# The first experts' results scattered to rows by choice and token, and read back by plain loads

## The reference

```python
x = x + L0_gnn(layernorm(x), edges)
xn = layernorm(x)
logits = xn @ gate_w + gate_b
# top 2 of 16 experts per row, weights from the two logits
y[q] = relu(xn @ w1[e_q] + b1[e_q]) @ w2[e_q] + b2[e_q]      # q = 0, 1
x = x + layernorm(xn + weight[0] * y[0] + weight[1] * y[1]) * gamma + beta
x = x + L1_gnn(layernorm(x), edges)
x = x + L1_ffn(layernorm(x))
```

## Time and profile before

| What | us |
|---|---|
| median of three runs | 3184.31 |
| span of the profiled execution (its own time; nothing around it is shown apart) | 3191.6 |
| first expert stage: its block's first work to the next block's | 1068 to 1427 |
| combining stage | 1427 to 1531 |
| second graph layer's aggregation begins | 1531 |
| second expert stage | 2703 to the end |

### The profile page before, as it was taken

The page is one execution under the profiler, slowest core; times in us unless marked ns, Lnnn a source line. Parts: engine busy times, 40 slices in busy tenths (PEclk is TensorE's granted clock), DMA queues, the critical chain, the costliest instruction groups (busy, mean ns, idle before and its releaser), DMA issues. The chain is left out here.

```text
span 3191.6 us, 47669 instructions
## 1 busy us (share of the span) xinstructions
PE 2342.0 (73%) x11533; PEld 1761.9 (55%) x11533; DVE 1710.0 (54%) x4544; ACT 1455.8 (46%) x3766; POOL 1992.3 (62%) x1963
## 2 busy tenths in 40 slices
PE   1549999989998389870366666666676666699997
PEld 1226666667686378660244444444444435599996
DVE  6659898857787500017566565666565655401110
ACT  0247676645564233323544444444444434355553
POOL 1647777667775677755677777777777760133332
PEclk9979999989998599995677776677766767799998
DMA  6657777578886666863777777777777752343223
GB/s 215 230 162 226 229 222 205 173 221 262 252 259 209 219 210 200 250 189 97 209 205 206 205 197 205 205 208 204 203 203 197 203 163 78 103 118 77 61 62 65
DMA packets 361528, 591.11 MB, mean 185 GB/s; under 512 B 81906, under 2 KB 234747, under 8 KB 359136
## 3 DMA queue, kind: packets, MB, share of 16 engines
q0 software_dynamic: 101648, 270.35, 32.0%
q1 hardware_dynamic: 241104, 295.49, 29.0%
q10 hardware_dynamic: 18544, 22.59, 2.2%
HBM read 428.77 MB, written 164.32 MB: 186 GB/s over the span
## 5 line engine op out<-in xcount | busy, mean ns | idle before, releaser
L659 POOL DMA_INDIRECT agg_r_rows<-h_table,parts_and_x x832 | 839.3, 1009 | 290.1 <-issue 217.9
L715 PE MATMUL agg_r_sums<-agg_r_rows,agg_r_onehot 128*128 128x257 f32 x1664 | 674.4, 554 | 382.0 <-DVE agg_r_rows L697 335.3
L715 PEld LDWEIGHTS agg_r_sums<-agg_r_rows,agg_r_onehot 128*128 128x128 f32 x1664 | 414.6, 272 | 624.5 <-issue 542.2
L626 ACT ACTIVATE agg_r_gap<-iota,parts_and_x 128x128 f32<-128x128 f32 x832 | 286.7, 392 | 469.5 <-PE agg_r_sums L715 443.5
L697 DVE TENSOR_TENSOR agg_r_rows<-agg_r_rows,agg_r_rel 128x514 f32<-128x514 f32 x416 | 290.6, 699 | 289.8 <-DMA agg_r_rows<-h_table,parts_and_x 288.4
L688 DVE TENSOR_TENSOR acc<-acc,agg_r_sums 128x257 f32 (+1 forms) x836 | 353.5, 423 | 147.5 <-issue 66.0
L1555 POOL DMA_INDIRECT rl_buf<-r_table,kinds x288 | 320.7, 1114 | 135.3 <-issue 75.4
L1956 PE MATMUL f_pH<-f_xT,f_w 128*128 128x128 f32 x2816 | 352.4, 283 | 36.0 <-DMA f_w<-in_L_ffn_w 24.4
L1956 PEld LDWEIGHTS f_pH<-f_xT,f_w 128*128 128x128 f32 x2816 | 337.3, 197 | 67.8 <-issue 28.3
L2041 ACT ACTIVATE f_hT<-f_pH,f_b 128x128 f32<-128x128 f32 x704 | 198.3, 373 | 298.4 <-PE f_pH L1956 298.0
L1975 PE MATMUL f_pY<-f_w,f_hT 128*128 128x256 f32 x1408 | 326.5, 382 | 8.3 <-DMA f_w<-in_L_ffn_w 8.0
(11 more groups left out here) (406 smaller groups left out, 3404.7 us busy)
## 6 DMA issues: line engine op xcount, KB each, us to landing
agg_r_rel<-relation_rows SPq DMA_DIRECT2D x404, 260.0 KB, 3.3
relation_rows<-rl_buf SPq DMA_DIRECT2D x144, 260.0 KB, 3.1
relation_rows<-rm_buf SPq DMA_DIRECT2D x132, 260.0 KB, 3.4
relation_rows<-f_rr_buf POOLq DMA_DIRECT2D x78, 260.0 KB, 3.2
agg_r_rows<-h_table,parts_and_x POOLq DMA_INDIRECT x832, 3.4
f_w<-in_L_ffn_W SPq DMA_DIRECT2D x18, 512.0 KB, 5.2
f_w<-in_L_ffn_W SPq DMA_DIRECT2D x9, 1024.0 KB, 4.9
f_ys<-f_yb SPq DMA_DIRECT2D x64, 128.0 KB
```

Source lines behind the costliest of these rows:

```text
L626: last = nc.scalar.activation(gap[:, n % HOT, t, :], c.iota[:, 0:P], ACT.Abs, bias=c.tab["b_near"][:, bass.ds(g * 2 + t, 1)])
L659: pool.indirect_dma_start(rows[:, n % SLOTS, t, :], None, table, bass.IndirectOffsetOnAxis(ap=indices[:, t:t + 1], axis=0)).then_inc(s_row ...
L715: last = nc.tensor.matmul(sums[:, (2 * n + t) % BANKS, 0:used], onehot[:, n % HOT, t, :], rows[:, n % SLOTS, t, 0:used], start=True, stop= ...
```

## The change

In the first mixture a slot's result now goes to the row (choice x 3200 + token) of a larger table `ys`, padding slots to rows of their own behind. The row numbers come out of the same matmuls as `token`: the second choice counts tiles from 25 on, and `token` subtracts 3200 again. GpSimd scatters each result with an indirect DMA without addition (`put_rows`), four tiles behind its gather; `yb` has four buffers, and VectorE's loop is written out. SyncE stores nothing any more in that stage. At the end GpSimd waits for its scatters, then does its two last relation stores. `combine_and_norm` reads `got` with twelve plain loads on SyncE ahead of gamma and beta. In both mixtures `home` is made right behind `token`.

```diff
-    ys = c.dram(f"{name}_ys", [NP + P if out is not None else tiles * P, D])
+    ys = c.dram(f"{name}_ys", [NP + P if out is not None else 2 * NP + tiles * P, D])
...
-    FC, Q, Y = nf // P, 4, 4 if out is not None else 2
+    FC, Q, Y = nf // P, 4, 4
...
                 with sp.Fori(1, tiles // 2 - 1) as i:
                     for s in range(2):
                         second(2 * i + s, s)
-                        if out is None:
-                            stored(i, s)
                         first(2 * i + 2 + s, s)
...
-                    hits = [P, NT, tiles]
+                    hits, first = [P, NT, tiles], q * NT if out is None else 0
...
-                v.tensor_scalar(token[:, :], token_f[:, :], 1.0, 0.0, ALU.subtract, ALU.max).then_inc(s_token, 1)
+                if out is None:
+                    v.tensor_scalar(home_f[:, :], token_f[:, :], float(NP), float(-NP), ALU.is_gt, ALU.mult)
+                    st.link(v.tensor_scalar(row_f[:, :], token_f[:, :], 1.0, 0.0, ALU.subtract, ALU.max))
+                    v.tensor_tensor(token[:, :], row_f[:, :], home_f[:, :], ALU.add).then_inc(s_token, 1)
...
+                v.scalar_tensor_tensor(home[:, :], token_f[:, :], -1.0, home_f[:, :], ALU.add, ALU.add).then_inc(s_home, 1)
...
-                    with dve.Fori(0, tiles // 2) as i:
...
+                    for t in range(tiles):
+                        e = dve.value_load(e_tab[0:1, 0, t:t + 1], min_val=0, max_val=ne - 1)
+                        dve.wait_ge(s_y, t + 3)
+                        if t >= Y:
+
+                            dve.wait_ge(s_added[t % Y], 16 * (t // Y))
+                        v.tensor_tensor(yb[:, t % Y, :], pY[t % 2][:, 0:D], b2s[:, bass.ds(e, 1), :].rearrange("p a d -> p (a d)"), ALU.add)\
+                            .then_inc(s_yb, 1)
...
+                def put_rows(t):
+                    pool.wait_ge(s_yb, t + 3)
+                    pool.sem_inc(s_ask, 1)
+                    pool.indirect_dma_start(ys, bass.IndirectOffsetOnAxis(ap=home[:, t:t + 1], axis=0), yb[:, t % Y, :], None).then_inc(s_added[t % Y], 16)
...
+                    if out is None and t >= Q:
+                        if t == Q:
+                            pool.wait_ge(s_home, 1)
+                        put_rows(t - Q)
...
-def gather_results(nc, c, name, k, ys, slot):
...
             @block.gpsimd
             def _(pool):
-                work(pool)
+                pool.memset(k.got[:, :, NT - 1, :], 0.0).then_inc(k.s_rest, 1)
...
             @block.sync
             def _(sp):
+                for i in range(NJ):
+                    full = J if i < NJ - 1 else J - 1
+                    for q in range(2):
+                        at = q * NP + i * J * P
+                        sp.dma_start(k.got[:, q, i * J:i * J + full, :], ys[at:at + full * P, :].rearrange("(t p) d -> p t d", p=P)).then_inc(k.s_got[i], 16)
+                sp.wait_ge(k.s_rest, 1)
+                for q in range(2):
+                    at = q * NP + (NT - 1) * P
+                    sp.dma_start(k.got[0:TAIL, q, NT - 1, :], ys[at:at + TAIL, :]).then_inc(k.s_got[NJ - 1], 16)
                 sp.dma_start(g[:, :], row(I["L0_ffn_gamma"])).then_inc(s_gb, 16)
                 sp.dma_start(b[:, :], row(I["L0_ffn_beta"])).then_inc(s_gb, 16)
...
-                    dve.wait_ge(k.s_got[i], 16 * 2 * J)
+                    dve.wait_ge(k.s_got[i], 32 if i < NJ - 1 else 64)
```

More of the change, by code:

```diff
@@ L1845, in feed_forward @@
             of_slot, two = k.sb(f"{name}_of_slot", [P, tiles]), k.sb(f"{name}_two", [P, tiles])
-            away, home_f, home = k.sb(f"{name}_away", [P, 1]), k.sb(f"{name}_home_f", [P, tiles]), k.sb(f"{name}_home", [P, tiles], I32)
             plain = k.sb(f"{name}_plain", [P, 2, D])
             shares_at = pY[1][:, D:D + 3 * tiles]
-            s_parts, s_shares, s_read, s_home, s_start, s_plain, s_copied = (k.sem(f"{name}_s{x}") for x in (
-                "parts", "shares", "read", "home", "start", "plain", "copied"))
-            s_added = [c.pool_sem(f"{name}_added{s}") for s in range(Y)]
+            s_parts, s_shares, s_read, s_start, s_plain, s_copied = (k.sem(f"{name}_s{x}") for x in (
+                "parts", "shares", "read", "start", "plain", "copied"))
+        away, home_f, home = k.sb(f"{name}_away", [P, 1]), k.sb(f"{name}_home_f", [P, tiles]), k.sb(f"{name}_home", [P, tiles], I32)
+        row_f = k.sb(f"{name}_row_f", [P, tiles])
+        s_home = k.sem(f"{name}_shome")
+        s_added = [c.pool_sem(f"{name}_added{s}") for s in range(Y)]
         loads = [(b1s[:, :, :], b1), (b2s[:, :, :], b2.rearrange("(a e) d -> a e d", a=1).to_broadcast([P, ne, D]))]
@@ L1861, in feed_forward @@
         s_x = [c.pool_sem(f"{name}_x{s}") for s in range(Q)]
-        s_st = [k.sem(f"{name}_st{s}") for s in range(2)]
         s_xt, s_xT, s_h, s_hT, s_y, s_yb, s_asked, s_ask = (
@@ L1893, in second @@
                     weights(sp, fresh, [(w2b[:, s, :, :].rearrange("p k f -> p (k f)"), w2[bass.ds(e, 1), :, :].rearrange("a p f -> p (a f)"), s_w2[s])])
-                def stored(i, s):
-                    sp.wait_ge(s_yb, 2 * i + s + 1)
-                    sp.dma_start(ys[bass.ds((i - 1) * P + s * (tiles // 2 * P), P), :], yb[:, s, :]).then_inc(s_st[s], 16)
                 for to, what in loads:
                     sp.dma_start(to, what, allow_slow_non_contiguous=True).then_inc(s_bias, 16)
-                if out is None:
-                    for s in range(2):
-                        sp.sem_inc(s_st[s], 16)
-                else:
+                if out is not None:
                     sp.dma_start(ys[0:NP, :].rearrange("(t p) d -> p t d", p=P), c.x[:, :, :]).then_inc(s_start, 16)
@@ L2127, in _ @@
                     for q in range(2):
-                        v.tensor_tensor(weight[:, q, :], top[:, :, q], small[:, 1, :], ALU.mult)
+                        last = v.tensor_tensor(weight[:, q, :], top[:, :, q], small[:, 1, :], ALU.mult)
+                    st.link(last)
                 else:
@@ L2212, in _ @@
                             asked += 1
-                if out is not None:
-                    for t in range(tiles - Q, tiles):
+                for t in range(tiles - Q, tiles):
+                    if out is not None:
                         add_rows(t)
+                    else:
+                        put_rows(t)
+                if out is None:
+                    for s in range(Y):
+                        pool.wait_ge(s_added[s], 16 * (tiles // Y))
                 if work:
@@ L2253, in rows, with combine_and_norm @@
         return last
-def gather_results(nc, c, name, k, ys, slot):
[L2258 to L2277, removed]
+def combine_and_norm(nc, c, name, I, ys, weight, xn, h_table):
     with Core(nc) as k:
-        work = gather_results(nc, c, name, k, ys, slot)
+        k.got = k.sb(f"{name}_got", [P, 2, NT, D])
+        k.s_got = [k.sem(f"{name}_got{i}") for i in range(NJ)]
+        k.s_rest = k.sem(f"{name}_rest")
         g, b = k.sb(f"{name}_gamma", [P, D]), k.sb(f"{name}_beta", [P, D])
```

31 lines of the change are left out of this document (16 added, 15 removed).

## The result

The change takes **3280.23 us** (median of 4 runs, 3277.68 to 3281.05), the kernel before beside it 3185.62: a ratio of 1.0288 with a 95% interval of 1.0267 to 1.0309, slower. The forecast was 3260 us, within 3236 to 3300. The profiled execution of the change took 3281.05 us with a span of 3279.3.

The account below looks back on a forecast made before the run. The prediction took GpSimd's issuing to bound the first expert stage. Its terms, 71.9 (scatters and stage end) + 4.1 (combining) - 0.6 (second expert stage) = +75.4 us, added to the median of 3184.31, gave 3260 us, range 3236 to 3300.

Parts of the forecast that it names:

- Term 1, the scatters: First expert stage: each scatter costs GpSimd 1.27 us with its gap, so gather 63 starts 74.3 us later.
- The adding scatter's price: Rival, first expert stage: a scatter costs what the second stage's adding one does, 1.57 us; time 3295, chance 0.13.
- lower bound of 0.89: First expert stage: lowest cost of a scatter in us, a plain store's 592 ns with the gap of 0.30.
- Term 1, the end of the stage: From the first expert stage's last token gather to the next block: 22.6 us instead of 25.0, so -2.4.
- with 0.4 us to the new block: End of the first expert stage: the next block begins 0.4 us after GpSimd's last relation stores land.
- Term 2, combining: Combining stage: beta waits behind the twelve loads, landing after 23 us; 100.1 us against 96.0, so +4.1.
- the lower end of 20: Combining stage: beta lands after some 20 us if the loads run at 386 GB/s; the other end was 28.
- Term 3: Second expert stage: home's instructions ahead of the weights let the first gather start about 0.6 us sooner, so -0.6.
- added to the median: Whole kernel: the terms' sum of +75.4 us was added to the median of 3184.31, giving 3260.
- beta not held up: Rival, combining stage: beta lands as before, -15.4 us, time 3240; chance 0.14 together with a scatter at the store's price.
- issue covered: Rival, first expert stage: GpSimd's scatter issue is hidden; combining gains, 3168, chance 0.03, or beta late, 3188, chance 0.03.
- the lower clock: Rival, first expert stage: TensorE, pausing in every tile, falls near 1.2 GHz; time 3415, chance 0.02.

Follow-up runs that it names:

- e2: The change with every scatter issued twice, the second into a table that nothing reads: 3359.05 us.
- e7: The change with each scatter replaced by a plain store from GpSimd in the order of slots: 3241.35 us.
- e8: The change with gamma and beta loaded first and the expert stage's 78 relation stores issued by SyncE instead of GpSimd: 3213.68 us, 1.0084 of before.
- e4: The change with GpSimd's two last relation stores ahead of its last four scatters, and SyncE waiting for the landings: 3275.83 us.
- e1: The change with the loads of gamma and beta ahead of the twelve loads of results: 3254.16 us, 1.0210 of before.
- e3: The kernel before with only the change's combining stage (twelve plain loads ahead of gamma and beta), no scatters: 3198.62 us, 1.0030 of before.
- e10: The change with each of the two loads of 53 rows cut into 48 rows and 5: 3275.03 us.
- e9: The kernel of e8 with 18 relation pairs moved from the expert stage into the combining stage: 3176.65 us, 0.9958 of before.
- e5: The change with 24 of the 78 relation pairs moved from the expert stage into the combining stage: 3226.18 us, 1.0122 of before.
- e6: The change with the edits of e1, e4 and e5 together: 3202.11 us, 1.0037 of before.

## Why the prediction was right

**Term 1, the scatters (forecast +74.3).** Right in mechanism and nearly in size: GpSimd's issue bounds the stage (e2, e7, e8), a scatter takes 0.995 + 0.30 = 1.30 us instead of 1.27, and gather 63 stands 365.4 us after gather 0, where the forecast's 1476.2 would be 362.9. (The 280.4 us from tile 4 to tile 63 that it counts are 60 gathers, not 64; the sum itself takes 59 steps and is right.) The adding scatter's price was the wrong neighbour, the token gather's the right one. My lower bound of 0.89 was wrongly made: it gave a plain store a gap that it does not have (e7). The Trainium skill (DMA: Bandwidth & Descriptors, Issuing engines are not separate DMA queues) says that to start DMAs from several engines saves only the time that starting them takes, which is usually small beside the transfer. Here it is not small: a scatter holds GpSimd for 1.30 us and lands 2.4 us after its issue, and 59 scatters between the first and the last token gather are 77 us, which nothing on GpSimd hides. The first scatter's wait (8 us more) and the waits for TensorE that went (9 us less) nearly cancel.

**Term 1, the end of the stage (forecast -2.4).** Wrong: +3.5, a miss of 5.9 us. The step that failed is "with 0.4 us to the new block": once GpSimd's last stores had landed, 9 us passed to the next block, 6.7 of them its drain and 2.2 behind the drain, while the landings themselves came some 3 us sooner than counted. Before, the drain ended ahead of SyncE's last landing and cost nothing; the change put it on the path by giving GpSimd the last work of the stage (e4).

**Term 2, combining (forecast +4.1).** The mechanism was right, shown by e1 and e3; its size was +6.5, because beta came 25.9 us in and not 23. The step that was off is the one behind the loads: the two loads of 53 rows hold one DMA engine (e10). The rule that the prediction cited from the Trainium skill (DMA: Bandwidth & Descriptors, Why a DMA increments its semaphore by 16 and not by 1) agrees; by it beta would have been at 24.5. That 23 is what e10 measures without the narrow loads is luck: the lower end of 20 was too low as well, since the loads ran at about 350 GB/s in the change, not at 386, and the 23 was chosen between two ends and not worked out.

**Term 3 (forecast -0.6)** can't be told from the spread of that stretch.

**The rest of the miss.** The medians differ by 94.6 us, the forecast by 75.4. The two profiled spans differ by 87.7: by the forecast's 75.4, and 2.5 (scatters), 5.9 (end), 2.4 (beta), 6.3 behind the combining stage and -4.8 ahead of the expert stage, the last two within the spread of the traces. The other 7 lie in "added to the median": the execution that I read was 7.3 above it, and the 5 us by which its expert stage was longer than in two other traces are waits that the change removes. A sum that counts on removing them can't be added to a median that may not hold them.

**Luck in the range.** The forecast was 20 us low. The range held the result by the room that it left for an adding scatter's price, and that price did not come; none of it was meant for the drain or for the slower loads.

**Rivals.** The adding scatter's price fell with the row of the 64 scatters (0.995 us against 1.574); beta not held up fell in the rows above; "issue covered" fell with e2. TensorE did not fall to the lower clock: from 1130 to 1400 us its granted clock was 0.95 of 2.4 GHz, against 0.97 before, and GpSimd's waits for it shrank to 0.3 us.

## What to carry to other kernels

Before work is moved onto a queue, ask whether that engine is idle in that stage: here 64 DMAs moved from SyncE, which took 0.35 us for each and had time to spare in a stage of over 300 us, to a GpSimd that issued end to end, and each cost its whole issue time. A small operand that everything waits for goes ahead of the bulk loads on its queue. And in a stage bound by one engine's issue, other work can be taken off it: 78 stores given to SyncE were worth 40 us (e1 to e8).

## What the runs showed that I had not expected

- On GpSimd an indirect DMA of 128 rows without addition costs its 0.95 to 1.0 us plus a gap of 0.30; a plain store 0.59 without a gap (e7).
- A block that GpSimd ends last stays open for 6.8 to 13.2 us behind its last DMA (e9 6.8, e4 9.0, change 11.2, e5 13.2); 5.2 (e9) to 9.8 us (e6) of that are GpSimd's drain, and where GpSimd waits for its own stores, their landing comes on top.
- SyncE's issue takes longer with loads in flight: the first of the ten large loads took 0.40 us, all ten 13.5, and the two of 53 rows with gamma behind them 6.0; with these cut into 48 and 5 rows, the same bytes held it 2.8 (e10).
